# Window attention scores as compact 10-column blocks, computed by column-group matmuls

## What is computed

```python
allf = jnp.stack(per_method, axis=-1)[..., perm]     # centre and (neighbour - centre), 4 methods
x16 = allf.reshape(B * N, k, total).astype(jnp.float16).astype(jnp.float32)
qh = x16.reshape(B * N, k, nheads, 32)
scores = jnp.einsum('bihd,bjhd->bhij', qh, qh) / np.sqrt(32)
attn = jax.nn.softmax(scores, axis=-1)
out = jnp.einsum('bhij,bjhd->bihd', attn, qh).reshape(B * N, k, total)
fused = out @ W_lin.T + b_lin
```

## Time and profile before

| | us |
|---|---|
| median of three runs | 2309.59 |
| span of the profiled execution (first to last instruction) | 2306.2 |
| PE, DVE, ACT, POOL busy over the span | 81%, 83%, 70%, 44% |
| layer 1 attention, from PE's first matmul to the start of the next stage (361.9 to 765.0) | 403.1 |
| layer 2 attention (968.6 to 1437.0) | 468.4 |

### The profile page before, as it was taken

One profiled execution on the slowest core, in us unless ns is written; L12 is line 12 of the kernel. 1 busy time (PEld: TensorE's weight loads), 2 busy tenths in 40 slices (PEclk: granted clock), 3 DMA queues, 4 the chain that ended last, 5 costly groups with the idle time before them and its releaser, 6 DMA issues. The chain is left out here.

```text
span 2306.2 us, 99850 instructions
## 1 busy us (share of the span) xinstructions
PE 1865.0 (81%) x37528; PEld 1286.8 (56%) x37528; DVE 1904.0 (83%) x3658; ACT 1616.7 (70%) x3249; POOL 1007.8 (44%) x995
## 2 busy tenths in 40 slices
PE   0296665888888566499999998677999999999967
PEld 0023335777777344389999997343554544454432
DVE  6798986999999599689989987783888888888865
ACT  0299985888888699689999998456555555555532
POOL 0000006999999200178888886001434444444311
PEclk9997668999999666699999999799999999999979
DMA  2103766666565167655555552212322322222210
GB/s 59 14 1 89 165 163 141 123 122 123 122 123 121 32 157 166 157 110 109 107 105 110 108 105 53 93 28 67 92 83 73 91 74 81 79 85 82 61 56 19
DMA packets 435513, 216.09 MB, mean 94 GB/s; under 512 B 301259, under 2 KB 404843, under 8 KB 435304
## 3 DMA queue, kind: packets, MB, share of 16 engines
q1 hardware_dynamic: 430120, 210.73, 39.2%
q10 hardware_dynamic: 5312, 4.31, 0.8%
HBM read 161.97 MB, written 52.96 MB: 93 GB/s over the span
## 5 line engine op out<-in xcount | busy, mean ns | idle before, releaser
L865 PE MATMUL pQ<-QM,QX 128*128 128x64 f16 (+1 forms) x5760 | 531.5, 216 | 2.1 <-issue 2.1
L863 PE MATMUL pQ<-neigh_lo,QX 128*128 128x32 f16 (+1 forms) x5760 | 519.8, 188 | 2.1 <-issue 2.1
L863 PEld LDWEIGHTS pQ<-neigh_lo,QX 128*128 128x128 f16 x5760 | 494.9, 103 | 5.4 <-issue 2.8
L865 PEld LDWEIGHTS pQ<-QM,QX 128*128 128x128 f16 x5760 | 486.9, 104 | 1.8 <-issue 1.7
L961 POOL TENSOR_TENSOR Dm<-Sc,mx 128x450 f32<-128x450 f32 x384 | 365.8, 953 | 77.8 <-DVE mx L921 77.8
L968 POOL TENSOR_TENSOR Ap<-E,R 128x450 f32<-128x450 f32 x384 | 366.0, 953 | 67.9 <-DVE R L934 57.5
L998 ACT ACTIVATE Vs<-pQ 128x480 f32<-128x480 f32 (+1 forms) x384 | 295.6, 770 | 4.7 <-PE pH L891 3.0
L930 DVE STREAM_TRANSPOSE AT<-Ap 128x480 f32<-128x480 f32 x384 | 259.3, 675 | 33.4 <-PE pH L891 10.9
L1963 POOL TENSOR_TENSOR MT<-cb,decay 128x512 f32 (+1 forms) x128 | 164.0, 1302 | 247.4 <-PEq L1731 150.6
L1011 ACT ACTIVATE E<-Dm 128x450 f32<-128x450 f32 x384 | 224.1, 584 | 60.1 <-POOL Dm L961 60.0
L921 DVE TENSOR_REDUCE mx<-Sc 128x15 f32<-128x450 f32 x384 | 224.0, 583 | 15.2 <-ACT Sc L992 15.1
(11 more groups left out here) (362 smaller groups left out, 3584.5 us busy)
## 6 DMA issues: line engine op xcount, KB each, us to landing
QM<-scratch_q SPq DMA_DIRECT2D x192, 240.0 KB, 2.7
QX<-scratch_q SPq DMA_DIRECT2D x768, 60.0 KB, 2.5
scratch_q<-QT SPq DMA_DIRECT2D x120, 360.0 KB, 4.8
Wg<-in_in_proj SPq DMA_DIRECT2D x64, 256.0 KB, 2.7
Wh<-in_in_proj SPq DMA_DIRECT2D x64, 256.0 KB, 2.8
Wo<-in_out_proj SPq DMA_DIRECT2D x64, 256.0 KB, 2.6
W_s<-in_in_proj SPq DMA_DIRECT2D x16, 256.0 KB, 2.7
CT<-scratch_c SPq DMA_DIRECT2D x192, 11.2 KB, 2.2
```

The lines of the kernel that those rows point to most:

```text
L863: nc.tensor.matmul(pQ[:, p, u // PB, o + 32:o + BW], qx[u], W["neigh_lo"][:, 0:O], start=False, stop=True, skip_group_check=True)
L865: last = nc.tensor.matmul(pQ[:, p, u // PB, o:o + BW], qx[u], qm[u], start=False, stop=True, skip_group_check=True)
```

## The change

The windows in DRAM are laid out anew (one block per unit, head and dimension; the 15 sub-blocks innermost), and are loaded for UT = 4 units at a time into a ring of NU = 4 (so 16 units), by seven DMAs and one for the centres. `QX` now holds a block-diagonal stationary: partitions 32n to 32n+31 hold the windows of token n in columns of token n and zero elsewhere, partitions 96 to 127 hold the windows of all three tokens. `QD` holds the three tokens' windows under each other. So a matmul over the first 96 rows gives each row its own token's 10 scores only: 10 columns a sub-block, 150 a unit, and no mask. Each head is a matmul of 30 output partitions in its own group of 32 columns of the array, so a sub-block takes four matmuls for the scores and four for the values. The step of PE's reads along the windows is 15 elements. The high and low halves of the weight are stacked on the partitions (`stack`), and one value matmul replaces two.

DVE takes the maximum and the difference from PSUM (`pS`); the copy `Sc` and POOL's difference go. POOL spreads the product back over three tokens: `RM = R x own` (45 values), then `Ap = E x RM`, with `own` the 0/1 pattern of the token that a row belongs to. All lags behind are one or two steps shorter, the loop body is U = 16 steps (11 passes).

```diff
-    U = RV = 8
-    NQ = 8
+    U = 16
+    NU = U // UT
+    RV = 8
...
-        QX = sb("QX", [128, NQ, SUBS // RES, 4, 32 * RES], F16)
-        QM = sb("QM", [128, NQ, SEG, GC], F16)
+        QX = sb("QX", [128, NU, UT * 4, PTS, GQ], F16)
+        QD = sb("QD", [128, NU, UT * 4, GQ], F16)
...
-        pQ = ps("pQ", [128, 2, NBK, 512])
+        pS = ps("pS", [128, 2, 512])
+        pV = ps("pV", [128, 2, 512 * (O // C)])
...
+        def windows(tile, w, y):
+            return tile[:, w, y, :, :].rearrange("p n (j u) -> p u (n j)", u=SUBS)
+        def dense(tile, w, y):
+            return tile[:, w, y, :].rearrange("p (j u) -> p u j", u=SUBS)
...
+                    for n in range(PTS):
+                        sp.dma_start(QX[32 * n:32 * n + 32, w, :, n, :], q16[:, span, n, :]).then_inc(q_in[w], 16)
+                        sp.dma_start(QD[32 * n:32 * n + 32, w, :, :], q16[:, span, n, :]).then_inc(q_in[w], 16)
+                    sp.dma_start(QX[96:128, w, :, :, :].rearrange("p y n x -> p y (n x)"),
+                                 q16[:, span, :, :].rearrange("d y n x -> d y (n x)")).then_inc(q_in[w], 16)
...
-                    for c in range(NBK):
-                        n = min(PB, SUBS - c * PB)
-                        nc.tensor.matmul(pQ[:, p, c, 0:n * BW].rearrange("p (s x) -> p s x", x=BW)[:, :, 0:32],
-                                         maskL[:, :], maskR[:, 0:32 * n],
-                                         start=True, stop=True)
                     for u in range(SUBS):
-                        o = (u % PB) * BW
-                        nc.tensor.matmul(pQ[:, p, u // PB, o + 32:o + BW], qx[u], W["neigh_lo"][:, 0:O],
-                                         start=False, stop=True, skip_group_check=True)
-                        last = nc.tensor.matmul(pQ[:, p, u // PB, o:o + BW], qx[u], qm[u],
-                                                start=False, stop=True, skip_group_check=True)
+                        for h in range(4):
+                            y = k % UT * 4 + h
+                            nc.tensor.matmul(pS[32 * h:32 * h + PTS * K, p, u * K:u * K + K],
+                                             windows(QX, w, y)[0:96, u], dense(QD, w, y)[0:96, u], start=True, stop=True)
+                        for h in range(4):
+                            y = k % UT * 4 + h
+                            last = nc.tensor.matmul(pV[32 * h:32 * h + PTS * K, p, u * O:u * O + O],
+                                                    windows(QX, w, y)[:, u], W["stack"][:, h, :], start=True, stop=True)
...
                 if at(1):
                     (t, _), p = at(1), (k - 1) % ND
-                    dve.wait_ge(scores_out, t + 3)
-                    dve.wait_ge(shifted, t + 1)
-                    v.tensor_reduce(mx[:, p, :], valid(Sc[:, p, :]), X, ALU.max).then_inc(max_ready, 1)
+                    dve.wait_ge(projected, t + 1 + U)
+                    v.tensor_reduce(mx[:, p, :], subs(pS[:, (k - 1) % 2, 0:GQ], K), X, ALU.max).then_inc(max_ready, 1)
...
+                    v.tensor_tensor(subs(Dm[:, p, :], K), subs(pS[:, (k - 1) % 2, 0:GQ], K),
+                                    mx[:, p, :].unsqueeze(2).to_broadcast([128, SUBS, K]),
+                                    ALU.subtract).then_inc(shifted, 1)
...
-                    nc.gpsimd.tensor_tensor(valid(A[:, p, :]), valid(E[:, p, :]),
-                                            R[:, p, :].unsqueeze(2).to_broadcast([128, SUBS, PTS * K]),
+                    nc.gpsimd.tensor_tensor(RM[:, p, :, :], R[:, p, :].unsqueeze(2).to_broadcast([128, SUBS, PTS]),
+                                            own[:, :].unsqueeze(1).to_broadcast([128, SUBS, PTS]),
+                                            ALU.mult).then_inc(rm_ready, 1)
+                    nc.gpsimd.tensor_tensor(subs(A[:, p, :], 32)[:, :, 0:PTS * K].rearrange("p s (n j) -> p s n j", n=PTS),
+                                            subs(E[:, p, :], K).unsqueeze(2).to_broadcast([128, SUBS, PTS, K]),
+                                            RM[:, p, :, :].unsqueeze(3).to_broadcast([128, SUBS, PTS, K]),
                                             ALU.mult).then_inc(probs, 1)
```

More of the change, by code:

```diff
@@ L206, in _ @@
                 pe.wait_ge(scaled, l + 1)
-                for side in range(2):
-                    last = nc.tensor.transpose(pw[:, l, 2 + side, 0:O],
-                                               eff[0:O, l, side, :, :].rearrange("p c m -> p (c m)"), ident[0:O, 0:O])
+                nc.tensor.transpose(pw[:, l, 2, 0:O], eff[0:O, l, :, :].rearrange("p c m -> p (c m)"), ident[0:O, 0:O])
+                for h in range(4):
+                    last = nc.tensor.transpose(pw[:, l, 3, h * O:h * O + O],
+                                               heads[0:O, l, h, :, :].rearrange("p a d -> p (a d)"), ident[0:O, 0:O])
                 last.then_inc(turned, 1)
@@ L838, in _ @@
         def _(pe):
-            pe.sem_inc(projected, NQ)
-            pe.sem_inc(mixed, RV // SL)
-            pe.wait_ge(const_in, 32)
+            pe.sem_inc(projected, U)
+            pe.sem_inc(mixed, U // SL)
+            pe.wait_ge(a_zeroed, 1)
+            none = A[:, 0:2, :].rearrange("p k x -> p (k x)").bitcast(F16)
+            for p in range(2):
+                nc.tensor.matmul(pS[:, p, :], none[:, 0:128], none[:, 0:512], start=True, stop=True)
+                for e in range(O // C):
+                    nc.tensor.matmul(pV[:, p, 512 * e:512 * e + 512], none[:, 0:128], none[:, 0:512], start=True, stop=True)
@@ L867, in scores @@
                     last.then_inc(projected, 1)
             def mix(k, at):
-                if at(5) and (k - 5) % SL == SL - 1:
-                    t, r = at(5)
-                    k3 = (k - 5) % U
-                    q, p, ring, first = pack(r, k3), k3 // SL % 2, k3 // RV, (k3 - SL + 1) % RV
+                if at(4) and (k - 4) % SL == SL - 1:
+                    t, r = at(4)
+                    k3 = (k - 4) % U
+                    q, p, w, first = pack(r, k3), k3 // SL % 2, k3 // UT, k3 - SL + 1
@@ L874, in mix @@
                     pe.wait_ge(copied, q + 1)
-                    for c in range(first // 2, (first + SL - 1) // 2 + 1):
-                        pe.wait_ge(c_in[c], (r * (U // RV) + ring) * 16 + 16)
+                    pe.wait_ge(c_in[w], r * 16 + 16)
                     strips = [(slot, half) for slot in range(SL) for half in range(O // 32)]
@@ L975, in _ @@
         def _(act):
-            act.dma_start(maskL[:, :], io["maskL"]).then_inc(const_in, 16)
-            act.dma_start(maskR[:, :], io["maskR"]).then_inc(const_in, 16)
-            for k in range(NQ // 2, NQ):
-                for c in range(1, SEG):
-                    nc.scalar.activation(wide(k, c), column(c), ACT.Copy).then_inc(wide_late, 1)
+            act.dma_start(own[:, :], io["own"]).then_inc(const_in, 16)
             act.sem_inc(vs_ready, 2)
-            act.sem_inc(scores_out, 2)
             act.sem_inc(exped, ND)
@@ L2322, in constants @@
     c["rows"] = np.stack([mid, 1 - 2.0 * mid, 1024.0 * low, 1 - 2.0 * low], 1).astype(np.float32)
-    c["maskL"] = np.array([[1024.0 * (i % 32 // K == n) * (n < PTS) for i in range(128)] for n in range(128)], np.float16)
-    c["maskR"] = np.tile(np.array([-1024.0 * (x // K != n) * (n < PTS) for n in range(128)], np.float16), (1, SUBS))
+    c["own"] = (x[:, None] // K == np.arange(PTS)[None, :]).astype(np.float32)
+    c["own"] = np.tile(c["own"], (4, 1))
     return c
```

270 lines of the change are left out of this document (119 added, 151 removed).

## The result

The changed kernel takes 3734.8 us (median of 4 runs, 3732.3 to 3736.0) against 2310.0 us (2307.3 to 2311.7): 1.617 times the time, 95% interval 1.615 to 1.619. The forecast was 3500 us, range 2950 to 3750. The direction and the mechanism came as forecast. The time is 235 us (7%) above the number, and 10 us above 3725, the upper end that the forecast's own terms gave; it is inside the stated range only because that was drawn up to 3750.

A forecast was written before the change was run, and what follows sets the result against it. PE's instruction fetch was taken as the bound: 532 packets x 3.8 = 2022 us, plus 26 filling and draining, replaces 871.5 us of attention; with +12 and +3 that is +1191 on 2306, so 3500 us, range 2950 to 3750.

The forecast's parts named there:

- The bound: Both attention stages: PE waits for its code, since bodies of 4832 and 5824 instructions are fetched again every pass; 2022 us.
- the fetch one packet ahead: PE's code: the next packet is asked for only when the one before comes into use; 4.05 us a packet measured.
- The number of packets: Both attention stages: 231 and 279 code packets, plus one broken packet for each of 11 passes a layer, 532.
- The price of a packet: PE's code fetch: 3.8 us a packet, the measured 4.05 less 0.2 for sparser data DMAs.
- The ends: Start of each attention layer: zeroing `QX` and landing 1.35 MB before a first matmul; +4 to +8 us, taken 6.
- `gather_windows` at 0: Gather stages: one added DVE instruction of 180 values stays under ACT's full pace; 0 to +5 us, taken 0.
- The +3 for `norm_and_keys`: `norm_and_keys` gains a few instructions; +3 us.
- The matmuls: PE in attention: 120 pairs a unit at 10.2 ns, 1.2 us; with the mix 1.6 or 2.0 us, hidden by the fetch.
- rival 3: PE in attention: column groups don't overlap for short matmuls, 30 ns each, code hidden behind; 3075 us, chance 0.06.
- DVE, ACT, POOL: Attention: their work per unit is hidden under the fetch, none above 60% busy; DVE 1.9 to 2.1 us nominal.
- Rival 1: PE's code fits or comes several packets ahead; layer 1 near 1.7 us a unit, layer 2 2.0; 2190 us, chance 0.12.

The follow-up runs named there:

- the cut kernel: The changed kernel with PE issuing score and value matmuls for only 8 of the 15 sub-blocks, passes of 16 units: 3130.0 us.
- With 11 sub-blocks: The kernel before with 16 units a pass in place of 8 and the mix cut to 11 of the 15 sub-blocks: 2443.4 us.
- the resident loop: Layer 1's loop in the changed kernel with 8 of 15 sub-blocks on PE and passes of 8 units in place of 16: 2863.3 us in all.
- the first shortening: The changed kernel, nothing left out, layer 2 in passes of 4 units in place of 16, windows loaded two units at a time: 3738.7 us.

## Why the prediction was right, and what it sized wrong

*The bound, and the fetch one packet ahead.* Both were right. That the fetch of a long body is the bound is shown from three sides: the body's length alone slows the kernel before (2562.6 us); halving the body with the same instructions takes layer 1 of the cut kernel from 3.9 to 2.26 us a unit; taking a quarter of PE's busy time in the two stages away gives 34 us. I took it that 4832 and 5824 don't stay; the limit is between 1640 and 1768 recorded instructions. (For "later passes have no such wait" I named rows of layer 1 only; in layer 2, from 1050 to 1400 us, PE has no wait at all.)

That the fetch runs one packet ahead is shown by the order of the packets and stops. In the rows of the result PE goes on at 703.20 and 706.95 us. q8's next packets start at 704.5 and 708.2, 1.3 us after each, with none between; the first has landed at 705.45, and PE goes on 1.5 us later. Over both loops, with the data quiet, the three parts are 1.2, 1.2 and 1.4 us (medians), 3.8 in all, and no two of 488 packets overlap. (With 11 sub-blocks, five pairs of 89 do.)

*The number of packets.* Forecast 532; the attention stages hold 248 + 296 = 544 (in before 7 + 12, where the forecast had the 15 of the first passes). The instruction count was exact to 1%. A pass breaks nearly two packets, not one (21 and 25 packets for 19.3 and 23.3 of 251). 12 x 3.8 = 46 us. The forecast's 4.6 and 5.5 us a unit leave out the broken packets that its sum has; with them they are 4.8 and 5.7, where 5.46 and 6.43 were measured.

*The price of a packet.* This term missed most. I took 3.8 us, below the measured 4.05, "since data DMAs will be sparser". They are sparser in share (0.45 against 0.61), but come in bursts of 1.4 MB per 4 units that keep the engines full for some 7 us; 4.16 and 4.11 us a packet were measured in the two passes, and 3.59 without the bursts. What is left of the attention's 203 us over forecast, 153, is put here: 544 packets at 4.08. The upper end, 554 packets at 4.05, would have been the better centre: I corrected a measured number by an argument without a row.

*The ends.* Forecast +6 a layer. PE's wait before its first score in layer 1:

```profile
387.61 0.23 PE L849 MATMUL pS<-QD,QX 96*30 96x10 f16 x4 [10.40 <-DMA QX<-scratch_q]
387.69 0.23 PE L853 MATMUL pV<-stack,QX 128*30 128x32 f16 x4
387.75 0.22 PE L849 MATMUL pS<-QD,QX 96*30 96x10 f16 x4
387.81 0.23 PE L853 MATMUL pV<-stack,QX 128*30 128x32 f16 x4
387.87 0.21 PE L849 MATMUL pS<-QD,QX 96*30 96x10 f16 x4
```

DVE's first memset was at 374.4, 13.2 us earlier; in before it was 5.1 (356.8 to 361.9). Layer 2 has 13.2 for 5.0. So +16 came for +12.

*`gather_windows` at 0.* Wrong, +34.6 us up to the two attention stages. (The +3 for `norm_and_keys` didn't show: the first subtraction of the gather is at 196.7 us before and 196.5 after.) A pass of four batches went from 39.0 to 43.5 us. In before ACT was full (39.0 of 39.0); now DVE is (43.02 of 43.50). I had priced only the added instruction of 180 values and not the new order of the old three. In before they read:

```profile
L599 DVE TENSOR_TENSOR QT<-ext,cen 128x1710 f16<-128x1710 f32 x96 | 180.6, 1936 | 28.4 <-ACT ext L687 23.8
```

540 ns more on each, three a batch, is 1.6 us a batch, and the added instruction takes 0.4. DVE was busy 35.7 of the 39.0 us, so it had only 0.8 a batch of room beside ACT. The terms (46 + 153 + 4, and 34.6 for the 3 forecast) and 1.4 in the rest are the 236 us between +1191 and +1427 of the spans. They add up by construction, since the 153 is what was left. All but the 3 us went the same way, so the number wasn't helped by errors that cancel.

*The matmuls.* From 387.75 to 387.87 us in the rows above PE starts 4 score and 4 value pairs: 15 ns a pair. That is half of the 30 ns of rival 3, which is out. It is half as much again as the 10.2 of the earlier trace rows; the granted clock was 0.50 here and 1.00 there, and how much of the difference is the clock isn't shown.

*DVE, ACT, POOL.* Forecast below 60% each: 49, 38 and 20% of the span. Maximum 315 ns for 270, `RM` 263 within 95 to 360. All hidden behind the fetch.

*Rival 1, code is no bound, 2190 us.* Its trigger didn't occur, but its price was wrong as well. I had scaled the DMA share to at most 1.77 us a unit; the resident loop showed the engines full at 2.26. So with these loads the change isn't faster in layer 1 on the other side of the fetch either. The DMA share of 0.61 was the row to doubt: it is an average over a pipeline that then waited for DVE, and a packet took longer in the resident loop (16 x 126.56 x 1.085 / 52780 = 42 ns against 16 x 359 x 0.599 / 151768 = 23 ns, for 372 and 285 bytes). The size alone doesn't make that: in the kernel that loads two units at a time a packet of 354 bytes took 27 ns (7.03 MB in 19840 packets at a share of 0.26 of 126.95 us).

The Trainium skill (Runtime: NRT & Kernel Launch, Instruction fetch mechanics) calls the cost of crossing a block "mostly hidden". The traces here don't agree: 251 small instructions take 3.09 us when resident at full clock, and their block comes only every 3.6 to 4.2 us. Whether it is hidden where a block takes longer to execute than that, no run here shows.

## What to carry to other kernels

Before splitting work into more, smaller matmuls, count what one pass of the loop issues on PE: the matmul and its weight load are two instructions, 1640 recorded ones stay, 1768 don't, and a longer body costs about 4 us for each 200 to 250 of its instructions in every pass, so long as these take PE less than that. The cure is a shorter pass, but check the rings, what SP waits for ahead of a load and the DMA's own bound with it: the first shortening gained nothing. Price a packet by its measured interval under the data traffic that will be there, and re-price every instruction whose access pattern changes, even where its count doesn't.

## What the runs showed of the hardware that I had not expected

A code packet's interval moves with data traffic: 3.6 to 3.9 us with the data queue nearly idle, 4.0 to 4.5 as the mean of a pass with a DMA share of 0.38 to 0.61, and up to 6.5 in a burst. The granted clock fell with the stops in the kernel before: 1.00 with the body resident, 0.86 where 5 us of 38 were lost. It was 0.50 through the changed kernel's fetching stages, but in its resident loops it was still only 0.58 to 0.68, so the stops aren't all of it. On DVE, fp16 writes 30 bytes apart cost 7486 ns for 1650 values where the same values written side by side cost 2476.
